# One expert block loop split into two halves of the batch, with GpSimd's transfers paced by TensorE

## The chip, the cores and the metric

The kernel runs on one core of one Trainium2 chip. Its engines are TensorE (PE; PEld is its weight load), VectorE (DVE), ScalarE (ACT), GpSimd (POOL) and SyncE (SP). The metric is the device time of one execution in microseconds, the median of a few runs. The profile's span is the time from the first to the last instruction, which is shorter than that time.

## The reference

Sixteen samples of 128 tokens by 128 features pass four layers. What is computed, in short (`b` is a sample):

```
# L0: feed-forward with the weights of one of 8 experts per sample, then a layer norm
h = gelu(x[b] @ Wi[e0[b]] + bi);  x1 = layernorm(h @ Wo[e0[b]] + bo + x[b]) * gamma[e0[b]] + beta[e0[b]]
# L1: norm over features, norm over tokens, FiLM by a small hypernetwork of the sample's subject
h = film(token_norm(layernorm(x1)));  probs = softmax(h @ router_w);  two best of 8 experts per token
y = sum over the two of gate * (relu(h @ exp_w1[e] + b1[e]) @ exp_w2[e] + b2[e]);  u = x1 + y
# L2: neighbouring features are rotated by an angle that belongs to the sample (cos, sin)
# L3: adapter of width 32: gelu(down(u)) through one of 16 expert matrices, up, + u, then a layer norm
```

Only L1's experts mix the samples: a token goes to two experts, so its 4,096 (token, expert) pairs are sorted by expert into blocks of 128 rows with one expert each.

## The kernel before, in words

The program of each engine is written out by hand in `@block.sync`, `@block.gpsimd`, `@block.scalar`, `@block.tensor` and `@block.vector`; an engine takes its instructions in the written order, and semaphores (`wait_ge`) hold it.

**Stage 1, L0 and the routing (0 to 97 us).** Sixteen samples in four groups of four. Per sample `up(b)` and `down(b)` are four matmuls each (8 records each, since a float32 matmul is two passes); ACT does the gelu between them. SP loads weights into six slots, and ACT loads x of group g+2 behind the gelu of the third sample of group g. `z_transposes`, `row_stats`, `film_factors`, `film_h`, `route`, `top2` and `store_rows` (which writes the routed input h to HBM) follow per group. When all four groups are through, DVE ranks and sorts the pairs (L1148 to L1216), one-hot matmuls on PE (`hot_in`, `hot_blk`) invert the sort, and `src_i`, `dest_i`, `exp_i` say which rows each block gathers, where its results go and whose weights it takes.

**Stage 2, the blocks (97 to 198 us).** The number of blocks is fixed at the most there can be, `BLOCKS` = 39. Per block POOL gathers 128 rows of h by an indirect DMA (L496), PE transposes them (L869), DVE copies them out of PSUM (L1285) and copies the block's first-layer weights from the table of all eight (L1291), PE does the first layer (`blk_up`), ACT the relu (L651), PE the second layer two blocks later (`blk_down`), DVE adds the bias (L1298), and POOL scatters the 128 rows to HBM in token order by a second indirect DMA (L504). POOL's order is gather n+7, then scatter n.

**Stage 3, L2 and L3 (198 to 237 us).** When every scatter has landed, SP and ACT fetch the rows of all tokens by eight direct DMAs of 256 KB. Four groups of four samples then pass `combine`, `l3_T`, `l3_down`, `l3_residual`, `l3_up`, `stats3`, the inverse root on POOL (L519), the shift on DVE (L1361), the norm on ACT (L691), and scale and shift on POOL or DVE; SP stores them.

## Time and profile before

| | |
|---|---|
| time of the runs, us | 265.86, 268.74, 272.72 (median 268.74) |
| span of the profiled execution, us | 237.1 |
| around the span, median less span, us | 31.6 (the page gives the profiled execution no time of its own) |
| busy, us: PE, PEld, DVE, ACT, POOL | 187.1, 157.3, 127.9, 100.3, 125.8 |
| bytes moved by DMA | 27.19 MB |
| first block's first layer starts, last block's second layer starts, us | 100.9, 196.3 |

PE is busy for 79% of the span, but stages have different limits, so the share says little: it is read stage by stage. A `DMA_INDIRECT` row on POOL is the time in which POOL prepares the transfer; the transfer itself ends later.

### The profile page before, as it was taken

What the parts mean: (1) busy time and instruction counts of PE and PEld (TensorE: products, weight loads), DVE (VectorE), ACT (ScalarE), POOL (GpSimd) and SP (SyncE); (2) the same over time, 40 slices, a digit from 0 to 9 for tenths busy, and PEclk for the clock granted to TensorE, in tenths of its full rate; (3) what the DMA queues carried; (4) which work ended last, traced back from release to release, by engine and by line L of the source; (5) the groups of instructions that cost most, each with busy time, mean ns of one, the idle gap of its engine ahead of it and who ended that gap; (6) DMA issues with size and microseconds to landing.
All of it is one profiled execution on the core that took longest, in us unless ns stands there. A gap on an engine that the chain in (4) does not pass through costs nothing.

```text
span 237.1 us, 5140 instructions
## 1 busy us (share of the span) xinstructions
PE 187.1 (79%) x1247; PEld 157.3 (66%) x1248; DVE 127.9 (54%) x540; ACT 100.3 (42%) x297; POOL 125.8 (53%) x133
## 2 busy tenths in 40 slices
PE   6699696998446593989999898888997999789900
PEld 5699495996343462478998787777776884268700
DVE  6101425679977699635776555553332320378761
ACT  3123169568221339135555434444443343025530
POOL 6002363655655002577777777777777774001960
PEclk9999889999755555599999999999999999979955
DMA  5999968931169910011111111111112310940113
GB/s 181 234 340 324 305 182 247 333 112 48 52 204 322 318 44 1 24 47 55 48 49 53 49 44 48 49 55 44 45 56 43 52 43 0 251 106 1 44 44 88
DMA packets 32790, 27.19 MB, mean 115 GB/s; under 512 B 3561, under 2 KB 28282, under 8 KB 32768
## 3 DMA queue, kind: packets, MB, share of 16 engines
q1 hardware_dynamic: 23648, 18.44, 26.1%
q0 software_dynamic: 2496, 4.66, 7.6%
q10 hardware_dynamic: 6624, 3.85, 5.7%
q8 instruction: 8, 0.13, 0.2%
q14 instruction: 14, 0.11, 0.1%
HBM read 22.73 MB, written 4.65 MB: 116 GB/s over the span
## 4 chain that ended last, share of the span: by engine, by line
PE 25%; POOL 22%; issue 17%; DMA 16%; DVE 15%; ACT 3%; ACTq 1%; DVEq 0%; POOLq 0%
PE bank L710 22%; POOL got L496 9%; DMA x_sb<-in_x 9%; POOL expert_rows L504 9%; DMA got<-h_rows,src_i 4%; DVE z L1058 2%; DMA w_place<-expert_rows 2%; POOL rstd L453 2%; DVE nmr L1361 2%; PE bank L717 1%; DVE hot_in L1190 1%; ACT act L597 1%; POOL rs L519 1%; DVE hot_blk L1188 1%; DVE st L1349 1%
## 5 line engine op out<-in xcount | busy, mean ns | idle before, releaser
L651 ACT ACTIVATE rows<-bank,small 128x128 f32<-128x128 f32 x156 | 44.5, 368 | 54.3 <-PE bank L710 54.3
L496 POOL DMA_INDIRECT got<-h_rows,src_i x39 | 38.8, 994 | 18.0 <-issue 9.7
L710 PE MATMUL bank<-gotT,rows 128*128 128x128 f32 x312 | 43.7, 283 | 5.6 <-issue 4.0
L504 POOL DMA_INDIRECT expert_rows<-rows,dest_i x39 | 39.9, 1022 | 12.4 <-issue 11.7
L710 PEld LDWEIGHTS bank<-gotT,rows 128*128 128x128 f32 x312 | 37.8, 191 | 10.8 <-issue 8.3
L710 PE MATMUL bank<-w,rows 128*128 x312 | 43.1, 282 | 1.2 <-issue 0.6
L710 PEld LDWEIGHTS bank<-w,rows 128*128 128x128 f32 x312 | 37.8, 191 | 2.8 <-issue 1.6
L597 ACT ACTIVATE act<-bank,small 128x128 f32<-128x128 f32 x64 | 18.1, 370 | 25.5 <-PE bank L710 25.3
L1298 DVE TENSOR_TENSOR rows<-bank,b_tab 128x128 f32<-128x128 f32 x39 | 11.4, 291 | 31.3 <-PE bank L710 30.3
L453 POOL TENSOR_TENSOR rstd<-veps,minus_half 128x4 f32<-128x4 f32 x12 | 12.3, 1022 | 25.5 <-DVE veps L1048 14.5
L1285 DVE COPY gotT<-bank 128x128 f32<-128x128 f32 x39 | 11.2, 288 | 17.5 <-PE bank L869 17.2
L710 PE MATMUL bank<-w_place,act 128*128 128x128 f32 x128 | 19.2, 298 | 1.4 <-ACT act L597 1.4
L710 PE MATMUL bank<-xT,w_place 128*128 128x128 f32 x128 | 20.0, 308 | 0.0
L710 PEld LDWEIGHTS bank<-xT,w_place 128*128 128x128 f32 x128 | 18.7, 224 | 0.7 <-issue 0.7
L710 PEld LDWEIGHTS bank<-w_place,act 128*128 128x128 f32 x128 | 17.3, 209 | 1.8 <-ACT act L597 1.8
L1291 DVE COPY rows<-w 128x512 f32 x39 | 17.6, 451 | 0.7 <-issue 0.7
L519 POOL TENSOR_TENSOR rs<-ve,minus_half 128x4 f32<-128x4 f32 x4 | 4.1, 1022 | 20.2 <-DVE ve L1354 20.1
L869 PE MATMUL bank<-ident,got 128*128 128x128 f32 x39 | 11.5, 294 | 3.1 <-DMA got<-h_rows,src_i 2.8
L710 PE MATMUL bank<-w,ident 128*128 128x512 f32 x26 | 13.9, 692 | 0.0
L710 PE MATMUL bank<-small,hT 128*128 128x8 f32 x32 | 5.7, 306 | 9.5 <-ACT hT L579 9.5
L1039 DVE BATCH_NORM_STATS2 st<-bank 128x6 f32<-128x128 f32 x32 | 7.1, 284 | 10.8 <-PE bank L710 9.0
L710 PEld LDWEIGHTS bank<-small,hT 128*128 128x128 f32 x32 | 5.5, 260 | 10.3 <-issue 10.3
(197 smaller groups left out, 263.5 us busy)
## 6 DMA issues: line engine op xcount, KB each, us to landing
w_place<-in_l_wi SPq DMA_DIRECT2D x16, 256.0 KB, 4.9
w_place<-in_l_wo SPq DMA_DIRECT2D x16, 256.0 KB, 5.9
w<-in_exp_w SPq DMA_DIRECT2D x16, 256.0 KB, 5.9
rows<-in_l_rows SPq DMA_DIRECT2D x16, 192.0 KB, 5.9
x_sb<-in_x ACTq DMA_DIRECT2D x4, 256.0 KB, 6.4
h_rows<-h_row ACTq DMA_DIRECT2D x4, 256.0 KB, 2.5
w_place<-expert_rows SPq DMA_DIRECT2D x4, 256.0 KB, 5.6
w_place<-expert_rows ACTq DMA_DIRECT2D x4, 256.0 KB, 6.3
```

Source lines behind the costliest of these rows:

```text
L453: g_.tensor_tensor(rstd[:, kind, :], veps[:, kind, :], minus_half[:, 0:GS], ALU.pow)\
L496: g_.indirect_dma_start(got[:, n % RING, :], None, h_dram, bass.IndirectOffsetOnAxis(ap=src_i[:, n:n + 1], axis=0))\
L504: g_.indirect_dma_start(y_dram, bass.IndirectOffsetOnAxis(ap=dest_i[:, n:n + 1], axis=0), y_blk[:, n % 4, :], None, bounds_check=TOPK * NR ...
L519: g_.tensor_tensor(rs3[:, g % 2, :], ve3[:, g % 2, :], minus_half[:, 0:GS], ALU.pow)\
L597: last = a_.activation(act0[:, b % 2, c, :], bank[1 + b % 2][:, c * P:(c + 1) * P], ACT.Gelu, bias=cols[:, bass.ds(e * FC + (R_BI + c), 1)])
L651: last = a_.activation(hid[:, k % 2, c, :], bank[k % 2][:, c * P:(c + 1) * P], ACT.Relu, bias=cols[:, bass.ds(e * FC + (R_B1 + c), 1)])
L710: return t_.matmul(out_, lhsT, rhs, start=start, stop=stop)
L869: t_.transpose(bank[6 + k % 2][:, 0:P], got[:, k % RING, :], ident[:]).then_inc(p_gT, 1)
L1039: do(v_.bn_stats(st[:, kind, k, :], src(k)))
L1285: v_.tensor_copy(gotT[:, n % 2, :], bank[6 + n % 2][:, 0:P]).then_inc(v_gT, 1)
L1291: v_.tensor_copy(w1_now[:, n % 2, :], w1[:, bass.ds(expert[n], 1), :].rearrange("p o f -> p (o f)"))\
L1298: v_.tensor_tensor(y_blk[:, n % 4, :], bank[4 + n % 2][:, 0:D], b2_tab[:, bass.ds(expert.pop(n), 1), :].rearrange("p o d -> p (o d)"), ALU ...
```

## The change

The whole kernel function is rewritten around two halves of eight samples. What it does:

- **Routing by half.** Samples 0 to 7 are routed, ranked and sorted on their own (`rank(0)`, `inverse(0)`, `sources(0)`), inside and right behind L0; samples 8 to 15 within the block loop of the first half, between its blocks. Each half has `BL` = 23 blocks, so there are `NBLK` = 46. The one-hot arrays are 368 wide in place of 1,248.
- **L0.** The bias is added in transposed form on POOL. DVE does the scale and shift of the first norm. x of groups 0 and 1 is loaded at the start, that of 2 and 3 behind the gelu of samples 0 and 4. 128 KB of L0's rows are loaded per sample in place of 192 KB.
- **Block loop.** First-layer weights come from HBM per block (SP, 256 KB, six buffers), so DVE copies none. ACT, not DVE, copies the transposed rows out of PSUM, behind the relus of the block before. The second layer is one block behind, not two. SP stores a block's 128 rows in block order by a plain DMA; POOL scatters nothing.
- **Fetch of the results.** POOL fetches them, 128 rows (one sample, one of its two experts) per indirect DMA: 16 for the first half within the second half's blocks, 16 for the second half in the tail. Gathers and fetches within the loop wait for `p_u` or `p_gT`, that is for PE's block (`beside_up`, `beside_rows`).
- **Tail.** The first half is two units of four samples, whose L3 runs within the loop (steps 37 to 46); the second half is four units of two samples. POOL does the first five inverse roots; the last is done by ACT (Sqrt) and DVE (`last_root`). The fetches of the units 4 and 5 wait for `p_uT`, PE's transposes of the units 2 and 3.
- L3's 16 expert matrices are multiplied once each and chosen by a register (`m_idx`), not once per sample.

The core of the diff (line breaks as in the file):

```diff
-            for n in range(AHEAD):
-                gather(n)
-            for n in range(BLOCKS):
-                if n + AHEAD < BLOCKS:
-                    gather(n + AHEAD)
-                scatter(n)
...
+            def beside_up(k):
+                pool.wait_ge(p_u, k + 1)
+
+            def beside_rows(k):
+                pool.wait_ge(p_gT, min(k + 3, NBLK))
+
+            for n in range(BL):
+                if n >= LEAD:
+                    beside_up(n - LEAD)
...
+                gather(n)
+                if n > BOTH:
+                    beside_rows(n - LEAD)
+                    gather(BL + n - BOTH - 1)
+                if n == 1:
+                    power(0, 3)
+                if n == 3:
+                    power(1, 2)
+                if n == 4:
+                    power(1, 3)
+                if n == 7:
+                    power(2, 2)
+                if n == 8:
+                    power(2, 3)
...
+            power3(0)
+            stored(1)
+            fetch(2)
+            power3(1)
+            fetch(3)
+            pool.wait_ge(p_uT, 3)
+            fetch(4)
+            power3(2)
+            pool.wait_ge(p_uT, 4)
+            fetch(5)
+            power3(3)
+            power3(4)
```

PE's order, with what it holds between the blocks (`rows_T` transposes gathered rows):

```diff
+            for k in range(NBLK + 1):
...
+                if k < NBLK:
+                    blk_up(k)
+                if k >= 1:
+                    blk_down(k - 1, e)
+                if k + 2 < NBLK:
+                    rows_T(k + 2)
+                if k == 2:
+                    z_transposes(2)
...
+                if k == 13:
+                    inverse(1)
...
+                if k == 37:
...
+                    l3_T(0)
+                if k == 38:
+                    l3_down(0)
+                    l3_residual(0)
+                if k == 39:
+                    l3_up(0)
...
+            def blk_down(n, e):
+                pe.wait_ge(a_hid, n + 1)
+                pe.wait_ge(a_gT, min(n + 3, NBLK))
```

ACT in the loop, and the last root:

```diff
+            for k in range(NBLK):
+                hidden(k, e)
...
+                if k + 2 < NBLK:
+                    transposed(k + 2)
...
+            a_.activation(warm[:], ones_row[:], ACT.Sqrt).then_inc(ac, 1)
+            norm3(NU - 2)
+            act.wait_ge(v_var3, NU)
+            a_.activation(sd3[:], ve3[:, there(NU - 1)], ACT.Sqrt).then_inc(a_sd3, 1)
```

**Order, place 1: GpSimd in the block loop.** `got<-h_rows` is a gather, `expert_rows<-rows` a scatter. Before, from the first scatter on:

```order
L504 DMA expert_rows<-rows,dest_i 4096x128 [waits v_y,v_idx]
L496 DMA got<-h_rows,src_i 128x128 [waits p_gT]
L504 DMA expert_rows<-rows,dest_i 4096x128 [waits v_y]
L496 DMA got<-h_rows,src_i 128x128 [waits p_gT]
L504 DMA expert_rows<-rows,dest_i 4096x128 [waits v_y]
```

With the change, the first blocks (`rstd` is an inverse root of the second half's norms):

```order
L485 DMA got<-h_rows,src_i 128x128 x2
L470 TENSOR_TENSOR rstd<-veps,minus_half 128x4 [waits v_var1]
L485 DMA got<-h_rows,src_i 128x128 [waits p_u]
L470 TENSOR_TENSOR rstd<-veps,minus_half 128x4 [waits v_var1]
L485 DMA got<-h_rows,src_i 128x128 [waits p_u] x3
L470 TENSOR_TENSOR rstd<-veps,minus_half 128x4 [waits v_var2]
L485 DMA got<-h_rows,src_i 128x128 [waits p_u]
L470 TENSOR_TENSOR rstd<-veps,minus_half 128x4 [waits v_var2]
L485 DMA got<-h_rows,src_i 128x128 [waits p_u] x7
```

The scatter is gone from this queue, and roots of the norms of samples 8 to 15 stand between the gathers.

**Order, place 2: GpSimd in the tail.** `w_place<-slot_rows` is a fetch of 128 rows. Before, the tail holds only this from the last scatters on:

```order
L504 DMA expert_rows<-rows,dest_i 4096x128 [waits v_y] x8
L519 TENSOR_TENSOR rs<-ve,minus_half 128x4 [waits v_var3,l_rows3]
L519 TENSOR_TENSOR rs<-ve,minus_half 128x4 [waits v_var3]
L528 TENSOR_TENSOR zg<-zg,rows 128x512 [waits a_z3]
L533 TENSOR_TENSOR z<-zg,rows 128x512 [waits gc]
```

With the change:

```order
L496 DMA w_place<-slot_rows,slot_i 128x128 [waits st_y2,st_y1,st_y3,st_y0,v_slot]
L496 DMA w_place<-slot_rows,slot_i 128x128 x3
L509 TENSOR_TENSOR rs<-ve,minus_half 128x4 [waits v_var3]
L496 DMA w_place<-slot_rows,slot_i 128x128 x4
L496 DMA w_place<-slot_rows,slot_i 128x128 [waits p_uT]
L496 DMA w_place<-slot_rows,slot_i 128x128 x3
L509 TENSOR_TENSOR rs<-ve,minus_half 128x2 [waits v_var3]
L496 DMA w_place<-slot_rows,slot_i 128x128 [waits p_uT]
L496 DMA w_place<-slot_rows,slot_i 128x128 x3
L509 TENSOR_TENSOR rs<-ve,minus_half 128x2 [waits v_var3] x2
```

Sixteen fetches stand in POOL's tail, where before SP and ACT issued eight larger ones; scale and shift left POOL.

**Order, place 3: TensorE around the ranking.** `small,hT` is the routing of a group, `ident,hT` its rows turned back, `both` the ranking; `xT,w_place` is `up`, `w_place,act` is `down`. Before, behind all of L0:

```order
L710 MATMUL bank<-small,w3v 32x128 x3
L710 MATMUL bank<-small,hT 128x8 [waits a_hT,v_top,a_hrow]
L710 MATMUL bank<-small,hT 128x8 [waits a_hT] x3
L798 MATMUL bank<-ident,hT 128x128 x4
L710 MATMUL bank<-both,behind 128x128 [waits v_top]
L710 MATMUL bank<-both,ones_bf 128x128
```

With the change, between the samples 13 and 15 of L0:

```order
L792 MATMUL bank<-ident,xbT 128x128 [waits g_xbo]
L792 MATMUL bank<-small,hT 128x8 [waits a_hT] x4
L792 MATMUL bank<-xT,w_place 128x128 [waits a_gelu,l_wi2,a_xT]
L792 MATMUL bank<-xT,w_place 128x128 x3
L792 MATMUL bank<-both,behind 128x64 [waits v_top]
L792 MATMUL bank<-both,ones_bf 128x64
L878 MATMUL bank<-ident,hT 128x128 x4
L792 MATMUL bank<-w_place,act 128x128 [waits l_wo1,a_gelu]
```

The ranking of the first half, which before came after all of L0, now stands in PE's queue ahead of the last samples of L0, with its wait for DVE.

## Rows read from the trace of the kernel before

**Rows 1.** The page's 40 slices of the span (5.93 us each): granted clock and GB/s.
```profile
PEclk9999889999755555599999999999999999979955
GB/s 181 234 340 324 305 182 247 333 112 48 52 204 322 318 44 1 24 47 55 48 49 53 49 44 48 49 55 44 45 56 43 52 43 0 251 106 1 44 44 88
```

**Rows 2.** Timeline of L0: start us, us, engine, line, form, [idle before <-releaser].
```profile
27.55 0.66 PE L717 MATMUL bank<-ident,x_sb 128*128 128x128 f32 x4 [2.24 <-DMA x_sb<-in_x]
...
29.55 1.91 PE L710 MATMUL bank<-w_place,act 128*128 128x128 f32 x8
...
34.14 1.06 PE L710 MATMUL bank<-w_place,act 128*128 128x128 f32 x8
...
50.72 0.96 PE L710 MATMUL bank<-small,hT 128*128 128x8 f32 x8
```

**Rows 3.** Timeline from the ranking to the first block.
```profile
83.14 0.42 DVE L1148 TENSOR_TENSOR_SCAN run<-scan_mask,bank 128x128 f32<-128x128 f32 x1 [0.49 <-PE bank L710]
...
88.32 2.67 DVE L1188 TENSOR_SCALAR hot_blk<-hot_tmp,part_f 128x1248 bf16<-128x1248 bf16 x1
...
90.91 3.33 DVE L1190 TENSOR_SCALAR hot_in<-col_bf,in_blk 128x128 bf16<-128x128 bf16 x20
...
97.04 1.21 POOL L496 DMA_INDIRECT got<-h_rows,src_i  x1 [6.39 <-DVE dest_i L1216]
...
100.92 1.16 PE L710 MATMUL bank<-gotT,rows 128*128 128x128 f32 x8 [0.38 <-DVE gotT L1285]
```

**Rows 4.** Timeline of PE, two first layers with eight blocks between their starts.
```profile
109.10 1.16 PE L710 MATMUL bank<-gotT,rows 128*128 128x128 f32 x8 [0.38 <-DVE gotT L1285]
...
124.86 1.06 PE L710 MATMUL bank<-gotT,rows 128*128 128x128 f32 x8
```

**Rows 5.** Timeline of the later loop: one turn of POOL, one relu.
```profile
138.41 0.98 POOL L496 DMA_INDIRECT got<-h_rows,src_i  x1 [0.30 <-issue]
...
139.70 1.01 POOL L504 DMA_INDIRECT expert_rows<-rows,dest_i  x1 [0.30 <-issue]
...
141.01 0.97 POOL L496 DMA_INDIRECT got<-h_rows,src_i  x1 [0.30 <-issue]
...
187.96 1.14 ACT L651 ACTIVATE rows<-bank,small 128x128 f32<-128x128 f32 x4 [1.67 <-PE bank L710]
```

**Rows 6.** Groups by line and shape: count | busy us, mean ns | idle before.
```profile
L579 ACT ACTIVATE hT<-bank,film 128x128 f32<-128x128 f32 x16 | 6.0, 462 | 12.0 <-DVE film L1102 12.0
L553 ACT ACTIVATE h_row<-bank 128x512 f32<-128x512 f32 x4 | 2.4, 601 | 6.0 <-PE bank L798 6.0
L665 ACT ACT_TABLE_LOAD x1 | 1.3, 1283 | 0.0
...
L1039 DVE BATCH_NORM_STATS2 st<-bank 128x6 f32<-128x128 f32 x32 | 7.1, 284 | 10.8 <-PE bank L710 9.0 <-PE bank L783 1.7
```

**Rows 7.** Timeline from the last block to the tail's first work.
```profile
196.33 1.15 PE L710 MATMUL bank<-w,rows 128*128 x8 [0.59 <-ACT rows L651]
...
198.69 0.98 POOL L504 DMA_INDIRECT expert_rows<-rows,dest_i  x1 [0.37 <-issue]
...
205.44 1.14 DVE L1333 SCALAR_TENSOR_TENSOR x_bo<-w_place,gates,x 128x128 f32<-128x128 f32 x4 [7.52 <-DMA w_place<-expert_rows]
```

**Rows 8.** Timeline of the tail, PE's transposes of two neighbouring groups, and its end.
```profile
212.68 0.60 PE L923 MATMUL bank<-ident,z 128*128 128x128 f32 x4
...
216.28 0.60 PE L923 MATMUL bank<-ident,z 128*128 128x128 f32 x4
...
226.78 1.02 POOL L519 TENSOR_TENSOR rs<-ve,minus_half 128x4 f32<-128x4 f32 x1 [1.39 <-DVE ve L1354]
...
231.49 0.69 DVE L1384 TENSOR_TENSOR z<-zg,rows 128x512 f32<-128x512 f32 x1
```

**Rows 9.** DMA issues of the page: count, KB each, median us from issue to landing.
```profile
got<-h_rows,src_i POOLq DMA_INDIRECT x39, 2.6
expert_rows<-rows,dest_i POOLq DMA_INDIRECT x39, 2.3
```

More of the change, by code:

```diff
@@ new lines, in conditional_layers_kernel @@
+        uT = xT[:].rearrange("p i c -> p (i c)")
+        a3 = a3[:].rearrange("p i c -> p (i c)")
+        place = lambda u: UNITS[u][0] % (2 * GS)
+        unit = lambda u: range(UNITS[u][1])
+        there = lambda u: slice(place(u), place(u) + UNITS[u][1])
+        wide = lambda u: slice(place(u) * P, (place(u) + UNITS[u][1]) * P)
+        earlier = lambda u: next(v for v in range(u - 1, -1, -1)
+                                 if place(v) <= place(u) < place(v) + UNITS[v][1]) if UNITS[u][0] >= 2 * GS else None
@@ L413, in _ @@
+            for u in range(NU):
+                sp.wait_ge(s_out[u], 16)
         @block.gpsimd
@@ new lines, in _ @@
+            ahead = 2 * BL - BOTH - 1
+            first_half = rows_of(0) + rows_of(1)
+            for k in range(BL - LEAD, NBLK - LEAD):
+                if k == FIRST_ROWS:
+                    stored(0)
+                i = k - FIRST_ROWS
+                gathers = 2 if i < 0 else k % 2 if i < 11 else 1
+                if gathers > 0 and ahead < NBLK:
+                    beside_up(k)
+                    gather(ahead)
+                    ahead += 1
+                if gathers > 1 and ahead < NBLK:
+                    beside_rows(k)
+                    gather(ahead)
+                    ahead += 1
+                if 0 <= i < len(first_half):
+                    beside_rows(k)
+                    fetch_row(*first_half[i])
@@ new lines, in norm3 @@
+            def norm3(u):
+                act.wait_ge(v_nmr3, u + 1)
+                if earlier(u) is not None:
+                    act.wait_ge(v_o3, earlier(u) + 1)
+                for k in unit(u):
+                    i = place(u) + k
+                    last = a_.activation(z3[:, i, :], o3_bank[u][:, k * P:(k + 1) * P], ACT.Identity,
+                                         bias=nmr3[:, i:i + 1], scale=rs3[:, i:i + 1])
+                last.then_inc(a_z3, 1)
+            act.wait_ge(v_exp, 1)
@@ L710, in mm, with keep_warm @@
                 return t_.matmul(out_, lhsT, rhs, start=start, stop=stop)
+            def keep_warm(n, place, rhs):
+                for _ in range(n):
+                    mm(place[:, 0:rhs.shape[1]], ident[:], rhs).then_inc(p_warm, 1)
             def x_transposes(g):
@@ L965, in _ @@
+            for u in range(2, NU):
+                l3_T(u)
+                l3_down(u)
+                l3_residual(u)
+                l3_up(u)
         @block.vector
@@ L1371, in last_scale_shift @@
[L1371 to L1379 removed]
+                if earlier(u) is not None:
+                    dve.wait_ge(p_uT, earlier(u) + 1)
@@ L1403 @@
+            shift_of_norm3(0)
+            scale_shift3(0)
+            stats3(1)
+            shift_of_norm3(1)
+            scale_shift3(1)
+            combine(2, unit(2))
+            for u in range(3, NU):
+                combine(u, unit(u))
+                stats3(u - 1)
+                shift_of_norm3(u - 1)
+                scale_shift3(u - 1)
+            stats3(NU - 1)
+            shift_of_norm3(NU - 1)
+            scale_shift3(NU - 1)
 def kernel(**inputs):
```

1505 lines of the change are left out of this document (803 added, 702 removed).

## The prediction, on record before the change was run

> **What bounds the kernel now.** I read the page's slices first, then the timelines of the stages, then the groups by line. The slices [rows 1] show three stages and, between the first two, a stretch from 62 to 100 us in which PE's clock is granted at 0.5 (1.2 instead of 2.4 GHz).
>
> L0 (to 58 us) is held by its loads and by x: PE waits for x of a group at 27.55 us [rows 2], with the same wait before the groups 1 and 3. Then comes a serial stretch: from the ranking at 83.14 to the first block at 100.92 us [rows 3] DVE sorts, and PE and the DMA queues have almost nothing.
>
> The block loop has two speeds. While gathers lie ready, PE sets the pace: eight blocks from 109.10 to 124.86 us, 1.97 us each [rows 4]. Later POOL sets it: a gather and a scatter cost 1.30 us each with the 0.3 us behind them, 2.60 us from gather to gather [rows 5]. From 100.9 to 197.5, the end of the last second layer [rows 3, 7], 39 blocks take 96.6 us.
>
> The tail takes 39.6 us to the span's end: the last scatter, eight fetches that let DVE start at 205.44 [rows 7], then four groups at 3.6 us [rows 8] and their norms.
>
> **The change, part by part, as three moments: loop start, loop end, end.**
>
> *Loop start, 100.9 before.* Clean L0: a sample costs PE 16 records, 1.9 to 2.1 us at full clock and 3.6 to 3.8 at half: 8 records take 1.06 against 1.91 [rows 2]. The early x removes PE's waits; DMA brings 0.5 MB of weights per sample at some 300 GB/s (1.75 us) [rows 1], just under PE. I take sample 3 at 21 us, sample 7 at 29. The chain of group 1 (three norms in a row, each a DVE part of 1.5 us and more, a root on POOL of 1.02 plus 0.3 [rows 8], then film, routing) is some 14 us: 43. Behind it stand group 2's statistics and two top-2, each a dozen small DVE instructions; I put the ranking at 48. PE waits in its queue for that ranking (place 3), which makes the last samples of L0 late, to 53; it doesn't matter, as DVE is later. Sorting: 7.8 us from 83.14 to 90.91 [rows 3], of which the wide arrays 4.1 (2.67 the second); at 368 of 1,248 columns that is 1.2, less what goes to ACT: 4.5. Then 16 one-hot rows at 0.17 (20 took 3.33), and experts and sources, 1.7 of the 2.8 between those rows' end and the first gather [rows 3]: `src_i` at 57. A gather is usable 3 us later (2.6 landing [rows 9]). PE also waits for `v_l0` of group 3, two scale steps like the four of 1.14 us [rows 7] and one set of statistics (four at 0.28 [rows 6] and their sums) behind the sources: 61.3. First block at **63**, gain 37.9. Bounds: 58 if none of PE's or ACT's in-order waits in L0 bite, 72 if they do. I stay nearer the lower one, since the steps between are rows.
>
> *Loop, 96.6 before.* 46 blocks in place of 39. POOL has one gather of 1.3 us per block and, in 16 of the blocks, a fetch of the same kind: never more than 2.6, on average under PE's time, and half 1's gathers run seven blocks ahead. So PE should pace: 46 x 1.97 = 90.6. What hides DVE's copies is nothing new, they are off (L1291) or on ACT. Fitted between the blocks on PE: token-norm transposes and rows back, 8 + 8 records at 0.12, 2; routing 2 x 0.96 [rows 2]; ranking 0.2; inversion 1.1; eight expert matrices 1.8; two L3 units of four at 3.6 [rows 8], 7.2; and register loads before each `l3_up` matmul, unseen in the trace beside another matmul: between 0 and 0.6 each, so 0 to 5; I take 2, as the loads of the block loop are hidden at 1.97. Together 16. Stalls: ACT's two film steps (4 x 0.46 [rows 6], 1.5 in the overlap) and two evacuations with their stores, 5 us in the blocks 5 to 8, of which 0.5 per block is slack: 3.5. In the same blocks POOL's roots wait for DVE, with later gathers behind them, whose slack is about 1.2 us; that falls together with ACT's 3.5. Sort and one-hot rows of half 1 on DVE, 4 us in blocks with 1.6 free, and PE waits for them in `inverse(1)`: 2.3. One table load, 1.3 [rows 6], less slack: 1.0. Half clock in the first blocks after PE's pause, as 62 to 100 us shows [rows 1]: 2.5. Stalls 9.3 (bounds 0 and 20). Loop 90.6 + 16 + 9.3 = **116**, cost 19.4; end at 179. The 256 KB of weights per block make 192 GB/s with gathers and stores, under the 300 that the slices show: nothing.
>
> *Tail, 39.6 before.* From the end E of the last second layer: bias and SP's store of 64 KB, 2.3 as the scatter's landing [rows 9], first fetch at E + 2.9. POOL then has 16 fetches at 1.30 (the gather's price [rows 5]) and three roots, 20.8 + 3.7: root 3 done at E + 27.4. The waits of the units 4 and 5 for `p_uT` come at E + 14.6 and 21.1; the transposes they name are done at about 14.3 and 18.2, so they cost nothing (bounds 0 and 3: they would bite if DVE's `combine(2)` came late). Then DVE in order: shift 0.3, norm 0.9, scale and shift 0.9, `combine(5)` 1.2: 30.8; statistics of unit 4 31.8, its root 33.1, norm behind ACT's Sqrt table load (1.3) 35.4, scale and shift 36.3; statistics 37.3; the last root on ACT and DVE 1.6, against 1.3 on POOL, but without its queue; shift, norm, scale, shift 2.1: 41.0. From the last DVE instruction (231.49 + 0.69 [rows 8]) to the span's end are 4.9. Tail **46**, cost 6.4 (bounds 41, if POOL's fetches overlap all else, and 50).
>
> **Sum:** 63 + 116 + 46 = 225 against the span of 237.1, -12.1. The median of the runs lies 31.6 above the span, and I leave that as it is: 268.74 - 12.1 = **256.6 us**. The runs themselves spread by 2.5%, so that about 2% is what can be told from no change: 263.4 and 274.1 are the marks.
>
> A table load took 1.28 us [rows 6], and two new ones lie on my path. The Trainium skill (ScalarE: Activation LUTs, What ACT_TABLE_LOAD costs) gives some 2.7 us for one: by it the sum would be 2.8 us more. The row decides.
>
> **Rivals.**
> 1. *It overlaps better.* Start at 58, none of the 9.3 us of stalls: 225 - 5 - 9.3 = 210.7, time 242.3. For it: PE held 1.97 with DVE far busier [rows 4]. Against: so many in-order waits. 0.15.
> 2. *The front eats it.* The chain of group 1 over four engines, each with L0 work in its queue, takes longer; PE's wait for the ranking (place 3) and ACT's film before the next gelu hold up the samples 11 to 15, and with them `v_l0`. Start at 72: time 265.6. The two halves then do not overlap as the change says. 0.13.
> 3. *A hand-off paces each block (the other side).* `down(k-1)` waits for ACT's copy of the rows of block k+1, and that copy stands behind four relus of 1.14 us [rows 5], which stand behind `up(k-1)`: relus 1.14, copy 0.35, two to three semaphore hops of 0.1 to 0.2 after a first layer of 1.06 come to 2.8 us, and PE allows 1.97 + 0.9. There is no slack to speak of. Before, the second layer was two blocks behind and DVE did the copy. Each 0.1 us of pitch costs 4.6; from 1.97 + (274.1 - 256.6)/46 = 2.35 us on it is slower. Between 2.12 and 2.35: 264 to 274 us, 0.09. At the 2.60 of the POOL-paced loop: 285.6 us, 0.06.
> 4. *The fetches of the tail follow one another.* If each had to land before the next, at 2.6 in place of 1.3 us, 16 of them cost 20.8 more: 277.4, slower. Against: gathers are issued every 1.3 us while each takes 2.6 to land [rows 5, 9]. 0.03.
>
> On rival 4: the Trainium skill (DMA: Bandwidth & Descriptors, Rules for kernel authors) says to join many small transfers into large ones, as those under 64 KB are mostly overhead; its fit of 2.0 us and the bytes gives 2.15 for 64 KB. By that rule the 16 small fetches are the wrong way round against the eight of 256 KB before.
>
> **Chances and range.** Forecast, with its own range 247 to 264: 0.54; the rivals 0.15, 0.13, 0.09 and 0.06, 0.03. Faster by over 2%: 0.51 of the forecast, 0.15, and half of rival 2, 0.72. Slower: 0.09. The rest, 0.19, is within 2%. The range of 243 to 269 leaves out 0.06 of rival 1, the 0.09 slower, and 0.04 of rival 3's lower part.
>
> **What would show it.** The first first layer of a block at 58 to 68 us; clock 0.5 for less than 10 us behind L0 in place of 38; starts of `blk_up` 1.9 to 2.1 us apart in blocks without other work, with no regular wait of PE for ACT's `gotT`; 46 blocks in 110 to 122 us; in the tail 16 `DMA_INDIRECT` rows at 1.3 us, POOL the longest part of the chain there, no wait for `p_uT`. I am wrong if PE's pitch is over 2.2 us, if the loop starts behind 70, or if the tail takes over 52.

## The result, and the profile after

| | before | after |
|---|---|---|
| time of the runs, us (median) | 265.86, 268.74, 272.72, 266.61 (267.68) | 242.84, 242.37, 241.35, 242.22 (242.30) |
| span, us | 259.7 to 271.2 (55 later runs of the same kernel) | 239.6 to 241.1 (the same runs) |
| profiled execution: span; loop start; loop; tail, us | 237.1; 100.9; 96.6; 39.6 | 241.1; 63.9; 136.1; 41.1 |

The ratio is 0.911 [0.907, 0.916], 8.9% faster; it leaves out executions in a slower state of the chip (before's 272.72 us), so it is not that of the two medians. Forecast were 256.6 us; 242.3 lies 0.7 us below the range. The profiled execution of after took 242.84 us, 1.7 more than its span.

Slices and groups of the page of after:

```profile
span 241.1 us, 5763 instructions
...
PEclk9999997999759999985999999999999997555555
...
GB/s 205 294 295 314 312 317 277 257 265 48 203 121 134 135 176 190 167 106 56 154 152 188 113 196 127 177 157 187 169 156 106 90 33 22 86 88 52 53 17 44
...
L485 POOL DMA_INDIRECT got<-h_rows,src_i x46 | 44.7, 972 | 42.6 <-PE bank L792 24.6
L496 POOL DMA_INDIRECT w_place<-slot_rows,slot_i x32 | 31.0, 968 | 35.8 <-PE bank L955 16.0
```

Against [rows 1] the stretch of 38 us at half clock is gone: the clock is at half in a piece of L0 (35.2 to 38.6 us), in two ahead of and in the first blocks (59.1 to 62.5 and 65.9 to 72.7), and in 106.9 to 113.7. In the tail it stays at half from 202.4 on, which is longer than before.

Timeline of after, the marks of the three stages:

```profile
63.94 1.06 PE L792 MATMUL bank<-gotT,w_now 128*128 128x128 f32 x8
...
200.49 0.32 SPq L414 DMA_DIRECT2D slot_rows<-y_blk  x1
...
202.84 1.02 POOL L496 DMA_INDIRECT w_place<-slot_rows,slot_i  x1 [13.62 <-DMA slot_rows<-y_blk]
...
223.81 0.95 POOL L496 DMA_INDIRECT w_place<-slot_rows,slot_i  x1 [0.30 <-issue]
...
224.77 0.73 POOL L509 TENSOR_TENSOR rs<-ve,minus_half 128x2 f32<-128x2 f32 x1
...
229.95 0.69 POOL L509 TENSOR_TENSOR rs<-ve,minus_half 128x2 f32<-128x2 f32 x1 [4.45 <-DVE ve L1401]
...
231.64 1.28 ACT L781 ACT_TABLE_LOAD   x1
...
238.34 0.42 DVE L1433 TENSOR_TENSOR z<-zg,rows 128x256 f32<-128x256 f32 x1
```

The start is close to what was forecast, and the tail 4.9 us shorter. The loop is 20 us longer: where fetches stand beside the gathers (blocks 28 to 35) a pair of blocks takes 4.9 us, 1.97 and some 2.95 by turns. One such turn of after:

```profile
157.36 0.95 POOL L496 DMA_INDIRECT w_place<-slot_rows,slot_i  x1 [0.87 <-PE bank L955]
...
158.16 1.06 PE L792 MATMUL bank<-w,hid 128*128 x8
158.47 1.15 ACT L706 ACTIVATE hid<-bank,small 128x128 f32<-128x128 f32 x4 [1.07 <-PE bank L792]
158.62 0.96 POOL L485 DMA_INDIRECT got<-h_rows,src_i  x1 [0.30 <-PE bank L792]
...
159.05 0.27 PE L955 MATMUL bank<-ident,got 128*128 128x128 f32 x1
...
159.16 1.06 PE L792 MATMUL bank<-gotT,w_now 128*128 128x128 f32 x8
160.24 0.28 ACT L696 ACTIVATE gotT<-bank 128x128 f32<-128x128 f32 x1 [0.62 <-PE bank L955]
160.31 0.29 DVE L1371 TENSOR_TENSOR y_blk<-bank,b_tab 128x128 f32<-128x128 f32 x1 [2.90 <-PE bank L792]
160.47 0.95 POOL L496 DMA_INDIRECT w_place<-slot_rows,slot_i  x1 [0.90 <-PE bank L955]
...
160.76 0.48 PE L792 MATMUL bank<-w,hid 128*128 x2 [0.54 <-ACT gotT L696]
```

Read it by ends, start plus time. PE's second layer ended at 159.22, but DVE adds its bias at 160.31. PE's transposition ended at 159.32; ACT, idle since 159.62, copies it at 160.24. Two engines wait for matmuls that ended some 1 us ago, and both go on together, 0.7 us behind the end (159.58) of a `DMA_INDIRECT` that stood 0.30 us behind another.

### The profile page after: what moved, and what is told of

Read it like the earlier page. It is cut to its first block, busy times and chain, and to the rows that moved or that the text cites. A ratio compares the mean times of both kernels' runs of the same rounds, so it can differ in the third digit from the quotient of the medians.

```text
span 241.1 us, 5763 instructions
## 1 busy us (share of the span) xinstructions
PE 192.6 (80%) x1390; PEld 171.7 (71%) x1390; DVE 106.4 (44%) x512; ACT 118.7 (49%) x373; POOL 100.9 (42%) x117
## 3 DMA queue, kind: packets, MB, share of 16 engines
q1 hardware_dynamic: 33419, 29.32, 42.9%
## 4 chain that ended last, share of the span: by engine, by line
PE 60%; issue 11%; ACT 10%; DVE 7%; POOL 3%; DMA 3%; another core or an unknown queue 3%; ACTq 2%; DVEq 0%; POOLq 0%
PE bank L792 54%; PE bank L955 3%; ACT hid L706 3%; DMA got<-h_rows,src_i 3%; POOL w_place L496 2%; ACT gotT L696 1%; PE bank L983 1%; DVE hot_in L1297 1%; ACT zg L729 1%; PE bank L878 1%; PE bank L803 1%; DVE st L1160 1%; DVE zg L1429 1%; ACTq L706 1%
## 5 line engine op out<-in xcount | busy, mean ns | idle before, releaser
L706 ACT ACTIVATE hid<-bank,small 128x128 f32<-128x128 f32 x184 | 52.6, 370 | 41.1 <-PE bank L792 32.3
L792 PE MATMUL bank<-w,hid 128*128 x368 | 52.2, 287 | 10.0 <-ACT gotT L696 5.5
L792 PE MATMUL bank<-gotT,w_now 128*128 128x128 f32 x368 | 53.6, 291 | 4.1 <-issue 1.5
L792 PEld LDWEIGHTS bank<-w,hid 128*128 128x128 f32 x368 | 46.4, 198 | 12.9 <-issue 12.8
L792 PEld LDWEIGHTS bank<-gotT,w_now 128*128 128x128 f32 x368 | 47.5, 202 | 9.5 <-issue 7.5
L1371 DVE TENSOR_TENSOR y_blk<-bank,b_tab 128x128 f32<-128x128 f32 x46 | 13.4, 291 | 78.3 <-PE bank L792 62.1
L496 POOL DMA_INDIRECT w_place<-slot_rows,slot_i x32 | 31.0, 968 | 35.8 <-PE bank L955 16.0
L643 ACT ACTIVATE act<-bank,small 128x128 f32<-128x128 f32 x64 | 18.2, 374 | 19.4 <-PE bank L792 19.4
L696 ACT ACTIVATE gotT<-bank 128x128 f32<-128x128 f32 x46 | 13.0, 282 | 17.4 <-PE bank L955 8.6
L983 PE MATMUL bank<-ident,xbT 128*128 128x128 f32 x16 | 3.9, 355 | 10.5 <-DVE xbT L1388 10.3
L792 PE MATMUL bank<-m,a 33*128 x32 | 9.7, 405 | 2.6 <-issue 1.4
L792 PE MATMUL bank<-ident 128*128 128x128 f32 x38 | 9.3, 430 | 1.9 <-POOL minus_half L446 1.9
```

Of the source, the lines that this page charges most:

```text
L496: g_.indirect_dma_start(y_in[:, t // GS, k, t % GS, :], None, y_dram[h], bass.IndirectOffsetOnAxis(ap=slot_i[:, h, j:j + 1], axis=0))\
L643: last = a_.activation(act0[:, b % 2, c, :], up_bank(b)[:, c * P:(c + 1) * P], ACT.Gelu, bias=cols[:, bass.ds(e * FC + (R_BI + c), 1)])
L696: a_.activation(gotT[:, n % TRING, :], got_bank(n), ACT.Copy).then_inc(a_gT, 1)
L706: last = a_.activation(hid[:, n % 2, c, :], up_bank(n)[:, c * P:(c + 1) * P], ACT.Relu, bias=cols[:, bass.ds(e * FC + (R_B1 + c), 1)])
L792: return t_.matmul(out_, lhsT, rhs, start=start, stop=stop)
L983: last = t_.transpose(uT_bank[u][:, k * P:(k + 1) * P], u_b[:, place(u) + k, :], ident[:])
```

## Where the 31.6 us were

The unchanged kernel, run again with a profile (page):

```profile
span 267.3 us, 5140 instructions
...
PEclk9979797998555569889879777977977989999985
```

It took 269.19 us, 1.9 more than its span. The page shown ahead of the prediction, span 237.1, stands for none of these: 55 later executions of the same kernel have spans of 259.7 to 271.2 us and times 1.8 to 3.1 above them. Its timeline, from the middle of the loop:

```profile
171.16 1.06 PE L710 MATMUL bank<-gotT,rows 128*128 128x128 f32 x8
...
172.05 0.27 PE L869 MATMUL bank<-ident,got 128*128 128x128 f32 x1
...
172.16 1.06 PE L710 MATMUL bank<-w,rows 128*128 x8
172.71 0.97 POOL L496 DMA_INDIRECT got<-h_rows,src_i  x1 [0.30 <-issue]
173.15 0.29 DVE L1298 TENSOR_TENSOR rows<-bank,b_tab 128x128 f32<-128x128 f32 x1 [2.38 <-remote]
...
174.24 1.08 POOL L504 DMA_INDIRECT expert_rows<-rows,dest_i  x1 [0.56 <-issue]
175.62 0.97 POOL L496 DMA_INDIRECT got<-h_rows,src_i  x1 [0.30 <-issue]
177.40 0.29 DVE L1285 COPY gotT<-bank 128x128 f32<-128x128 f32 x1 [2.96 <-remote]
...
177.75 1.65 PE L710 MATMUL bank<-gotT,rows 128*128 128x128 f32 x6 [4.53 <-DVE gotT L1285]
177.75 1.14 ACT L651 ACTIVATE rows<-bank,small 128x128 f32<-128x128 f32 x4 [3.40 <-remote]
```

PE ended the transposition at 172.32, and DVE copies it at 177.40, 5.1 us later; PE then waits for that copy. DVE and ACT had both waited about 3 us for something that the view can't name ("remote"), and they go on 0.8 and 1.2 us behind the end (176.59) of POOL's last indirect DMA. The trace records the changes of three of PE's semaphores, for matmuls that ended at 172.21, 172.32 and 173.21, together at 177.34 to 177.47; DVE's copy starts 0.02 us behind its own. Eight blocks in a row of [rows 4] took 1.97 us each; here a block takes 3.27 on average, and the loop 127.6 us in place of 96.6. Start (101.7) and tail (38.0) agree with the page shown. This profiled execution was among the slowest on its chip; c1 below, with the same instructions on POOL and a time of 263.74 us, has a loop of 126.1 us and some 60 of 110 completions late.

To count this, each matmul that counts up a semaphore was matched with the first recorded change of that semaphore behind its end. **Late** means over 0.3 us; gaps over 8 us are left out. A change that was not recorded counts as late, too. The columns are: late ones among those that end during an indirect DMA on POOL or up to 0.6 us behind it, then those that end elsewhere; the loop's length in us; PE and POOL busy in 60 us of it (110 to 170 us for kernels like before, 120 to 180 for those like after) and the granted clock there.

```
kernel                        late near   elsewhere   loop     PE    POOL  clock
before, page shown             2 of 123    0 of 88    96.6   55.09  45.99  1.00
before again (c0)             56 of 112    0 of 99   127.6   45.87  35.23  0.83
after                         60 of 102    1 of 124  136.1   50.76  35.88  1.00
before, plain DMAs (e1)               -    0 of 211   77.8   59.55   0.00  1.00
before, gathers plain (f1)    10 of 66     0 of 145   79.5   59.29  30.06  1.00
before, paced (g1)            58 of 116    1 of 95   120.6   41.56  36.95  0.92
after, plain DMAs (e2)                -    0 of 228  124.5   56.54   1.01  1.00
after, half the fetches (f2)  48 of 79     0 of 146  130.7   53.97  21.51  1.00
after, not paced (e3)         20 of 39     0 of 176  179.0   32.81  32.11  0.81
```

How many can be missing records? The three semaphores that PE counts up in the blocks have 120 changes in e1, which misses none, and 118 in the page shown, whose two late ones are just these two; 110 in c0, 114 in f1; 141 in e2, which misses none, and 119 in after. So at most 10 of the 56 in c0 and 22 of the 60 in after are no more than that, but up to 6 of the 10 in f1. The waiting engines show it without these records: DVE's bias and the copy of the transposed rows start over 0.5 us behind both their matmul and their engine's own last instruction in 27 of 78 cases in c0 and 17 of 92 in after, in 4 of 78 in f1, and in none in the page shown, e1 and e2.

In e3 the longest gaps are over 8 us and so are not counted.

I call a completion that is seen late so a **hold**. In c0 it strikes 47 of 68 when the indirect DMA starts under 0.5 us behind the one before it, and none of 12 when over 2 us lie between. In after these are 35 of 42 and 4 of 17.

## The experiments

Times are compared by ratios with before on the same chip, whose median was 263 to 270 us from one chip to another.

**First: is it the page of before, or something in the program?** Theory A: hardware loops (`Fori`) on PE and ACT. Theory B: rows that the scatter skips as out of bounds. For the changed kernel, rival 3: ACT's copy stands too late.

```diff
c1_inbounds  (padding rows get spare rows of their own, all in bounds)
-            do(v_.tensor_scalar(pad[:], dest[:], float(P), FAR, ALU.is_lt, ALU.mult))
+            do(v_.scalar_tensor_tensor(out=pad[:], in0=dest[:], scalar=float(P), in1=spare[:],
+                                       op0=ALU.is_lt, op1=ALU.mult))
c2_unrolled  (the same on ACT)
-            with pe.Fori(0, LOOPS) as turn:
+            for turn in range(LOOPS):
c3_copy_first
                 hidden(k, e)
+                if k + 2 < NBLK:
+                    transposed(k + 2)
...
-                if k + 2 < NBLK:
-                    transposed(k + 2)
```

> The kernel before, unchanged, for the time and the span of the same executions. Theory (a fixed part outside the span): every execution has a span near 237 and a time near 267, so that 30 us lie outside the span of each. Rival (the profiled execution was a lucky one): the spans of these executions are near 266, 1 to 2 us below their times, as in the changed kernel, and the profile of 237.1 stood for none of the timed runs.

> The kernel before, but the 896 rows of padding are scattered to spare rows of HBM inside the bounds instead of being dropped past them; same instructions on POOL, same bound check. Theory (dropped rows cost time that the span does not show): the time falls by 25 to 30 us to 238 to 243 with the span still near 237. Rival (they cost nothing, the 30 us come from elsewhere): 266 to 270, within 1% of before; the 896 more rows written (0.46 MB) can make it 0 to 3 us slower.

> The kernel before, but the two hardware loops of three turns (8 blocks each) on PE and ACT are written out, as the changed kernel has them. Theory (the loops cost time, 3 turns on two engines, that the span does not show): the time falls by 20 to 30 us to 238 to 248. Rival (dropped rows or something else): 266 to 270, within 1% of before.

> The changed kernel, but ACT copies the transposed rows of block k+2 right behind the relus of block k, ahead of its register load for the next block, which the trace shows as 0.5 to 0.6 us between the relus and the copy. Theory (the loop's pitch of 2.46 is set by relus, register load, copy and then the second layer, which waits for the copy): pitch falls to 2.2 to 2.3, loop 136 to 126 to 131, time 232 to 238. Rival (the loop is PE's own work with its register loads, the wait for the copy only takes the place of another): pitch stays at 2.4 or above, time 241 to 243.

Measured: c0 269.19 and 261.82 us against 265.23 of 19 runs, each with a span 1.9 or 2.0 us below its time. c1 1.000 [0.995, 1.006], loop 126.1. c2 0.991 [0.986, 0.997], loop 123.5. c3 243.76, 0.922 [0.918, 0.926], loop 135.0. So neither theory A nor B is it, and moving the copy in ACT's order gains nothing.

**Second: PE's register load of the block's expert.** It stands ahead of each pair of layers, and the first late completion of c0 comes with the first such load.

```diff
d1_before_no_loads, d3_after_no_loads (d4: the same for the choice of L3's matrices)
-                if k >= 1:
-                    e = pe.value_load(exp_i[0:1, k - 1:k], min_val=0, max_val=E1 - 1)
+                e = 0
d2_before_loads_unused
+                e = 0
...
+                    pe.value_load(exp_i[0:1, k - 1:k], min_val=0, max_val=E1 - 1)
+                    blk_down(0, k - 1, 0)
```

> The kernel before, without PE's register load of the block's expert in front of each second layer: PE takes the second-layer weights of expert 0 in all blocks (the output is wrong by that, nothing else changes). Theory (PE's register loads are what makes PE's completions reach the other engines 1 to 6 us late, as in the c0_before trace from the first such load at 104.7 us on, and what takes the 25 us by which that span is over the profile's 237): time 237 to 242, pitch of the loop 2.6 us, POOL's. Rival (the late completions come from the loop's load on PE or on the queues, whatever PE's loads): 262 to 268, as before.

> As d1_before_no_loads, with weights of expert 0 at a fixed address, but PE still does the register load in front of each second layer and leaves its value unused. Theory (the load itself does it): 261 to 268, as before. Rival (the address out of a register, with its register instructions between the matmuls, does it): 237 to 243.

> The changed kernel without PE's register loads in the blocks (second-layer weights of expert 0 in all blocks, so the output is wrong by that). Theory (late completions behind register loads): pitch falls from 2.46 to 2.0 to 2.1, PE's own; loop 136 to 114 to 120, time 220 to 228. Rival (ACT's relus and the copy behind them pace the block): pitch 2.3 or above, time over 235.

> As d3_after_no_loads, and also no register load in front of the last matmul of each L3 sample (it takes matrix 0 for all). Theory: 24 loads fewer within the tail and 8 in the loop; 1 to 4 us under d3_after_no_loads, as PE waits for itself in the tail only behind ACT and the fetches. Rival (POOL's 16 fetches set the tail): the same as d3_after_no_loads within 1 us.

Measured: d1 0.989 [0.984, 0.994], d2 0.983 [0.971, 0.995], loops 129.6 and 129.0: the loads do not make before slow, against the theory. d3 237.87, 0.883 [0.876, 0.890]; d4 236.73, 0.880 [0.873, 0.887], loops 130.0 and 129.9. In the changed kernel the block loop's loads cost 4 to 8 us (242.3 less 237.9, from different chips; 136.1 less 130.0 of loop; or 0.911 less 0.883 of before), which the forecast had counted as hidden. In e2 below, with the loads and without indirect DMAs, plain blocks do take 2.1 us on average (the seven from 28 on), so the loads seem to cost only beside those.

**Third: the indirect DMAs, and the change's waits.**

```diff
e1_before_plain, e2_after_plain  (f1_before_one: gathers alone, in before)
-                g_.indirect_dma_start(got[:, n % RING, :], None, h_dram,
-                                      bass.IndirectOffsetOnAxis(ap=src_i[:, n:n + 1], axis=0))\
+                sp.dma_start(got[:, n % RING, :], h_dram[m * P:(m + 1) * P]).then_inc(gat[n % RING], 16)
...
e3_after_unpaced
             def beside_up(k):
-                pool.wait_ge(p_u, k + 1)
+                pass
             def beside_rows(k):
-                pool.wait_ge(p_gT, min(k + 3, NBLK))
+                pass
e4_after_dve_copy
+                dve.wait_ge(p_gT, n + 1)
...
+                v_.tensor_copy(gotT[:, n % TRING, :], got_bank(n)).then_inc(a_gT, 1)
```

> The kernel before, with every gather and scatter of 64 KB issued by SP as a plain DMA of 128 rows in order in place of POOL's indirect one: the same bytes, the same waits, no DMA_INDIRECT anywhere (blocks get the wrong rows, so the output is wrong by that; the addresses of the one-hot sort are computed but not used). Theory (a completion of PE that falls into a DMA_INDIRECT of POOL, or up to 0.6 us behind one, is held until that is over; of c0_before's completions 56 of 112 in such stretches are 0.3 to 6 us late, and 0 of 99 outside): no completion over 0.3 us late, pitch PE's own 1.97 to 2.1, span 101 + 78 to 82 + 38 to 41, time 219 to 226. Rival (they are late for another reason, as PE's own load): still tens of late ones, pitch 2.4 or more, time over 235.

> The changed kernel, with all gathers and fetches as plain DMAs on SP (wrong rows in the blocks and in L3, the output is wrong by that). Theory: as in e1_before_plain no late completions; pitch of the loop from 2.46 to 2.0 to 2.15, loop 136 to 114 to 122, tail 41 to 33 to 40, time 216 to 229. Rival (ACT's relus and copy, or PE's own work, pace the block): pitch 2.3 or more, loop over 128, time over 232.

> The changed kernel without the waits of gathers and in-loop fetches for PE's block (beside_up and beside_rows empty); what is left are the ring's own waits. Theory (each DMA_INDIRECT holds PE's completions; paced, one begins just behind a completion, when the next is 1 us off, back to back they hold for several us): 247 to 262, half of the gain on before gone. Rival (the waits only delay gathers): 238 to 244.

> The changed kernel, but DVE in place of ACT copies the transposed rows out of PSUM, right behind the bias of the block before, so that no copy stands behind relus. Theory (held completions set the pitch): 238 to 243, pitch 2.35 or more. Rival (the hand-off over ACT sets it, rival 3 of the prediction): pitch 2.1 to 2.25, time 226 to 234.

Measured: **e1 208.66 to 213.47 us** against a median of 263.29 (about 0.80, without an interval), faster than either range. Its loop takes 77.8 us, 1.99 a block on average. e2 227.97, 0.859 [0.846, 0.872], in the theory's range of time, but its loop of 124.5 us is 2.5 over the theory's. **e3 281.47, 1.066 [1.055, 1.077]**: without the two waits the change is 6.6% slower than before, and 19 us over the theory's range. e4 245.04, 0.927 [0.912, 0.942], 2 us over the theory's range and far from the rival's: no gain. The windows of e1 and e3 (us; busy us and count of PE, PEld, DVE, ACT, POOL; clock; DMA share; GB/s):

```profile
110.00:170.00 60.00, 59.55 (x528) 58.90 (x528) 36.45 (x127) 35.41 (x124) 0.00 (x0) 1.00 0.23 65
```

```profile
120.00:180.00 60.00, 32.81 (x235) 29.83 (x233) 9.95 (x31) 19.85 (x68) 32.11 (x34) 0.81 0.41 106
```

PE is busy for 59.6 of 60 us where POOL issues nothing, and for 32.8 where POOL issues as it likes. The timeline of e3 shows the waits:

```profile
168.15 1.13 PE L792 MATMUL bank<-gotT,w_now 128*128 128x128 f32 x8 [0.16 <-issue]
168.41 0.96 POOL L496 DMA_INDIRECT w_place<-slot_rows,slot_i  x1 [0.30 <-issue]
...
172.03 1.14 ACT L706 ACTIVATE hid<-bank,small 128x128 f32<-128x128 f32 x4 [5.55 <-remote]
...
178.50 0.96 POOL L496 DMA_INDIRECT w_place<-slot_rows,slot_i  x1 [0.30 <-issue]
179.09 0.29 DVE L1371 TENSOR_TENSOR y_blk<-bank,b_tab 128x128 f32<-128x128 f32 x1 [12.18 <-remote]
...
180.40 0.28 ACT L696 ACTIVATE gotT<-bank 128x128 f32<-128x128 f32 x1 [7.24 <-remote]
...
180.93 2.07 PE L792 MATMUL bank<-w,hid 128*128 x8 [11.65 <-ACT gotT L696]
```

While POOL issues ten and more without a pause, PE, ACT and DVE wait for each other: 11.65 us on PE. Three blocks of this loop took 14.9, 14.9 and 16.6 us.

**Fourth: how many, and how close.**

```diff
f2_after_fewer  (the first half's 16 fetches inside the loop go)
-                if 0 <= i < len(first_half):
-                    beside_rows(k)
-                    fetch_row(*first_half[i])
f3_after_inverse_later  (f4_after_lag2: this, and the second layer two blocks behind)
-                if k == 13:
+                if k == 15:
                     inverse(1)
g1_before_paced
                 if n + AHEAD < BLOCKS:
+                    pool.wait_ge(p_u, n + 3)
                     gather(n + AHEAD)
g2_after_gap
                     beside_up(k)
+                    ch.settle()
+                    ch.do(g_.tensor_tensor(spare[:], spare[:], minus_half[:], ALU.pow))
                     gather(ahead)
```

> The kernel before with one DMA_INDIRECT per block in place of two: the scatters stay on POOL, the gathers are SP's plain DMAs as in e1_before_plain (the blocks get wrong rows, the output is wrong by that). Theory (a DMA_INDIRECT holds PE's completions until 0.6 us behind its end, no longer; a scatter starts 0.35 us behind a second layer, so it holds the next first layer and transposition for some 0.9 us, of which the relus, waiting for the second layer anyway, hide the first): pitch 1.93 plus 0.4, loop 88 to 95, time 224 to 233. Rival (the cost goes by the number of transfers, half of the way between e1_before_plain's loop of 77.8 and c0_before's 127.6): loop 103, time 238 to 243.

> The changed kernel without the 16 fetches of the first half inside the loop (L3 of the first half reads what lies in the buffer, so the output is wrong by that). Theory (a block with two DMA_INDIRECTs costs 3.0 us, one with one 1.9): the blocks 25 to 40 hold one or none, and the loop loses 16 x 0.5 = 8 us of its 136, time 232 to 236. Rival (the fetches are hidden): 240 to 243.

> The changed kernel with PE's inversion of the second half's sort, and DVE's use of it, at block 15 in place of 13 and 14; nothing left out. Theory (the step of 8.0 us between two first layers there, in e2_after_plain without any DMA_INDIRECT too, is PE waiting in its queue for DVE's one-hot rows; two blocks later they are there): 235 to 239. Rival (the wait only moves, since POOL's gathers of the second half and DVE are as late as before): 241 to 244.

> f3_after_inverse_later, and the second layer two blocks behind the first in place of one, with a third buffer for the relus' output, and DVE in place of ACT copying the transposed rows; nothing left out. Theory (a held first layer then finds a block of slack before PE waits for its relus; the transpositions and second layers, held 0.6 us, have it already): 4 to 9 us less than f3_after_inverse_later, 227 to 234. Rival (the held completions stop PE elsewhere, at the copies): within 2 us of f3_after_inverse_later.

> The kernel before with one part of the change alone: each gather in the blocks also waits for the first layer of the block three behind it in POOL's order (p_u), as the changed kernel's gathers do; nothing left out. Theory (what costs is a DMA_INDIRECT right behind another, and a block of 1.97 us with a gather and a scatter of 1.0 us each has no room to keep them apart: the scatter comes 0.3 to 0.5 us behind the gather): no real gain, pitch 3.0 to 3.3, 260 to 270. Rival (a paced start is enough, however many there are): pitch 2.3 to 2.7, 240 to 252.

> The changed kernel with one idle root (a TENSOR_TENSOR of 1.0 us on four columns) on POOL in front of each gather that waits for a first layer, from block 19 on, so that the gather starts 1.3 to 1.6 us behind the DMA_INDIRECT ahead of it and not 0.3; same transfers, nothing left out. Theory (the second of two back to back is what holds completions; far apart they are nearly free, as f1_before_one shows): late completions from 60 to 20 to 40, pairs of blocks from 4.9 to 4.0 to 4.5 us, time 235 to 240. Rival (a completion is held by any DMA_INDIRECT that it falls into, so two per block cost the same apart; or POOL's added time makes gathers late): 241 to 247.

Measured: **f1 215.93, 0.791 [0.782, 0.800]**: with one indirect DMA per block left on POOL, 1.9 us from start to start, the loop takes 79.5 us, less than either range, and a copy follows its transposition 0.27 us behind its end. So the first indirect DMA of a block costs almost nothing and the second some 46 us over the loop (126.1 in c1): the theory's price per DMA was wrong, and so was the rival's share by number. Timeline of f1:

```profile
142.31 0.27 PE L866 MATMUL bank<-ident,got 128*128 128x128 f32 x1
...
142.79 0.99 POOL L506 DMA_INDIRECT expert_rows<-rows,dest_i  x1 [0.91 <-DVE rows L1295]
142.85 0.28 DVE L1282 COPY gotT<-bank 128x128 f32<-128x128 f32 x1
...
144.87 0.99 POOL L506 DMA_INDIRECT expert_rows<-rows,dest_i  x1 [1.09 <-DVE rows L1295]
```

f2 238.55, 0.881 [0.874, 0.888], loop 130.7, between the two ranges. What f1 left were scatters; that gathers alone behave alike is seen in the traces of after, f2 and e2. The seven blocks from 28 on take 17.7 us in after (a gather every second block, a fetch in each), 14.9 in f2 (the gathers alone) and 14.9 in e2 (none); the ten from 8 on, with one gather each in most, 29.7 in after and 29.2 in e2.

f3 243.27, 0.897 [0.890, 0.904]: PE's wait for the one-hot rows is gone (the inversion runs through in 0.56 us, and blocks 13 to 15 take 10.4 us in place of after's 13.7), but the gathers of the second half now come late, and blocks 17 and 18 take 8.0 in place of 5.0; the loop took 135.3. (The step of 8.0 us in its expectation is 7.1 in the trace.) f4 246.32, 0.906 [0.897, 0.915], with more late completions (73 of 103), is outside both its ranges and no gain. **g1 260.72, 0.969 [0.962, 0.976]**: the change's idea alone, one wait in front of before's gathers, is worth 3.1%. It still has 58 of 116 completions late, and a block takes 3.09 us on average, as its theory said. g2 243.43, 0.906 [0.899, 0.912], in the rival's range. Its timeline of POOL:

```profile
146.57 1.02 POOL L488 DMA_INDIRECT got<-h_rows,src_i  x1 [0.20 <-POOL spare L570]
147.90 0.94 POOL L499 DMA_INDIRECT w_place<-slot_rows,slot_i  x1 [0.30 <-issue]
149.15 0.94 POOL L499 DMA_INDIRECT w_place<-slot_rows,slot_i  x1 [0.30 <-issue]
150.12 1.04 POOL L570 TENSOR_TENSOR spare<-spare,minus_half 128x4 f32<-128x4 f32 x1
```

The idle root only regrouped them: now the fetches follow the gather and each other by 0.30 us. Where 1.2 to 2 us did lie between two of them, 15 of 25 completions were still late. So that close neighbours are struck most is a count, and that the distance is the cause is not shown.

None of c3, e4, f3, f4 and g2 is clearly ahead of the change: in us all lie behind it (243.3 to 246.3 against 242.3), and by the ratio only f3 lies ahead (0.897 against 0.911), on another chip, where the changed kernel itself was not timed.

## Why the prediction was wrong in size and right in direction

**The step that failed** is "The median of the runs lies 31.6 above the span, and I leave that as it is". Measured, 1.7 to 3.1 us lie above the span. Of the 31.6, some 29.8 were loop time of before that the page shown did not have. The forecast took them over as a constant: 225 + 31.6 = 256.6, against 240.5 + 1.8 = 242.3, so 29.8 too much there and 15.5 too little inside the span. That the miss is 14.3 us and not 30 is luck: the two errors stand against each other. The Trainium skill (Runtime: NRT & Kernel Launch, The ~15µs preamble/postamble breakdown) gives a gap of about 6.2 us that is the same for every kernel, but the other way round, the profile's total above the reported time. Here the time is above the span, so no run shows that figure; that the difference hardly changes from kernel to kernel the runs do show, and 31.6 was the sign that page and times belonged to different executions.

**Against what was timed**, each stage changed so (c0's marks to after's; c1's loop of 126.1 would make it 1.5 us more): start 101.7 to 63.9, a gain of 37.8 (forecast 37.9); loop 127.6 to 136.1, a cost of 8.5 (forecast 19.4); tail 38.0 to 41.1, a cost of 3.1 (forecast 6.4). The sum is -26.2 where -12.1 was forecast. Of the 14.1 between them, 10.9 are the loop's: before lost 48 to 50 us to the indirect DMAs (c1 and c0 against e1), after only 11.6 (136.1 against 124.5 in e2). So the change was worth more than forecast because the loop that it replaced was 31 us longer than the page shown had it.

**Start, 63**: 63.9. The path held, and not only its end: sample 7 is through L0 at 29.9 us (forecast 29), the ranking starts on PE at 50.1 (48), `src_i` is done at 58.8 (57). Rival 2 (72) is out. Not foreseen was that PE waits 3.49 us for a gelu behind four table loads in a row (28.3 to 34.2 us). Pieces of half clock add up to 10.3 us around the first blocks, about as said.

**Loop, 116**: 136.1, the worst term. 11.6 of the 20.1 go without the indirect DMAs (e2); no row of the page shown has them. The other 8.5 are in e2 too: it has 35.7 us over 46 x 1.93, where the fitted work and stalls were put at 25.3. The two steps around `inverse(1)` took 7.1 and 3.8 us, 7.0 over two plain ones, where 3.4 were counted: ACT's share of the one-hot rows waits for DVE's sort with the relus and the copy behind it (1.93 us on PE), PE then waits for DVE's one-hot columns, and runs at half clock behind that (104.0 to 110.8). Timeline of e2:

```profile
101.48 1.15 PE L779 MATMUL bank<-w,hid 128*128 x8 [1.93 <-ACT gotT L683]
...
104.23 0.34 PE L779 MATMUL bank<-hot_blk,hot_in 128*128 128x46 bf16 x4 [1.30 <-DVE hot_in L1284]
...
105.64 2.05 PE L779 MATMUL bank<-gotT,w_now 128*128 128x128 f32 x8 [0.42 <-issue]
```

L3's steps (37 to 39, 4.0 us each in e2) were about as forecast. The sign that starts would lie 1.9 to 2.1 us apart, with no regular wait for `gotT`, did not come true: 1.97 and 2.95 by turns, with that wait.

**Rival 3** named that wait, and for the wrong reason. ACT's copy was not late behind the relus: in the turn shown it started 0.62 us behind them and 0.92 behind PE's transposition. Putting it first (c3) or on DVE (e4) gained nothing. **Rival 1**'s time, 242.3, is the measured one to the digit, by luck: neither its start of 58 nor its loop without stalls came true. **Rival 4** is out: the fetches went at 1.25 us each, so the 16 small ones did not have the price that the prediction's sentence on small transfers feared; the tail grew by 3.1 us in all.

**Tail, 46**: 41.1. With E at 200.0 the first fetch is at E + 2.8 (forecast 2.9). Sixteen fetches at 1.25 and two-column roots at 0.73 (1.02 was the price of four columns) end root 3 at E + 25.5 in place of 27.4. The waits for `p_uT` cost nothing, as forecast: fetch(4) starts at 214.22, and its transposes ran from 212.79 to 213.45. The last DVE instruction ended at E + 38.7 (41.0), and then 2.3 us passed, not 4.9; the last store is half as large, but that this is the reason is not shown. The table load was 1.28 us again, as [rows 6] had it, and ACT's next instruction started 0.01 us behind it (232.93), so nothing here shows the 2.7 us that the prediction cites against it.

## What stays open

It is open why the execution shown ahead of the prediction had no holds (its 2 of 123 are missing records) with the same program. It has 4,099 recorded semaphore changes against 3,388 in c0, and this goes together in all traces looked at: without holds the recording is complete or nearly so (4,099, and 4,100 in e1), with them it is not (3,296 in g1, 3,667 even in f1; in the changed kernel 5,152 in e2 and 3,669 in after). So a rival is left untested: that the recording of the events itself holds the engines, or that both have one cause. Every timed run here has a span of its own and so none is known to be free of it. Nor is it known which part of an indirect DMA on POOL holds PE's completions back: e1 and e2 change the issuing engine, the kind of transfer and the order of the rows at once. In c0 the first late one belongs to a matmul that started at 104.7 us, 6.6 us behind the first gather, and none in L0.

## What to carry to other kernels

Before adding up anything, compare the span of the profile with the times of the runs: if much more lies between them than in other runs (here 1.7 to 3.1 us in every one), the profile shows another execution, and a change is worth something else in the timed ones. Indirect DMAs on GpSimd can cost the engines around them several times their own 1.0 us: look for waits on matmuls that ended long ago, with both waiters released just behind a run of `DMA_INDIRECT`. What helped here was to issue fewer of them, one per block in place of two, and to tie each to the progress of the engine it feeds.

## What the runs showed of the hardware

In the loop of before about half of PE's completions that fell near an indirect DMA on POOL were recorded 0.3 to over 5 us late, and were usually released 0.6 to 1.0 us behind the end of the last one. Without indirect DMAs there was none in 439. With one per block the loop took 79.5 us, with none 77.8. The price of two per block was 48 to 50 us of a loop of 126 to 128, and 42.9 us between the paced and the unpaced form of the changed kernel (136.1 and 179.0). The Trainium skill (SBUF — State Buffer, SBUF: two separate sides) says that PE and ACT never wait on anyone for their access, and that only the port pair shared by VectorE and GpSimd makes engines wait for each other. The matmuls themselves did keep their 0.13 us a record here, which fits; but the rule says nothing on completions. Taken as a rule on time it would let GpSimd's DMAs cost PE and ACT nothing, where the loops of c1 and e1 differ by 48 us.
